# Projecting the second attention's queries, keys and values inside the first expert layer's loop, through one PSUM bank

## Chip, cores and metric

One NeuronCore of one Trainium2 chip runs the kernel. The metric is the device time of one execution in microseconds; the kernel before takes 853.91 us, the median of three runs (852.01 to 854.15).

## What is computed

4096 tokens (16 sequences of 256) of 128 features go through four layers, each with a residual and a normalisation behind it:

```python
x = _layernorm(x + _L0_attn_ref(x, ...))   # softmax attention, 16 heads of 8
x = _layernorm(x + _L0_ffn_ref(x, ...))    # 8 experts of 128, top 2, gated
x = _layernorm(x + _L1_attn_ref(x, ...))   # causal linear attention, Taylor feature map
x = _layernorm(x + _L1_ffn_ref(x, ...))    # 8 experts, each takes 512 tokens
```

The change touches the second and the third line. The second, for every token (clipping of gate and up left out):

```python
gate, up = gu[..., ::2], gu[..., 1::2]             # gu = x @ gate_up_proj + bias
act = (up + 1.0) * gate * sigmoid(gate * ALPHA)
out = sum over experts of w[token, e] * (act @ down_proj[e] + down_proj_bias[e])
```

The third begins with three projections of the normalised result: `q = x @ Wq.T` and `k = x @ Wk.T` (256 columns each, 16 heads of 16) and `v = x @ Wv.T` (128 columns).

## The kernel before

Tokens are processed in 8 chunks of 512 (`NCH`, `CH`), each of 4 tiles of 128 tokens. `xn` holds all tokens in SBUF, a tile per 128 columns. Every stage is a block with one instruction list per engine; each list runs strictly in the order written, and semaphores tie the lists together.

`expert_layer0` (line 339) runs 64 units, `n = 8 * chunk + expert`. On TensorE a unit is `expand(n)` (up, L466, then gate, L468, into two double-buffered banks) and `reduce(n - 2)` (the down projection of the unit two before, L478). At given units `turn_weights` and `add_bias` are put behind that, for the bias of the down projection; they use `ps_r` and `ps_d` in turn. ScalarE reads up (`take_up`, L701) and gate with the activation (`take_gate`, L706). VectorE's iteration n is `clip(n)`, `activate(n)` (L579), `accumulate(n - 2)` (L590, four instructions that add the weighted result into `xn`), and at some n `add_bias`, `row_stats` and `merge_rows` for the normalisation. GpSimd normalises a few tiles at the start of the stage (L746).

`project_layer1` (line 775) is the next stage. Per chunk: VectorE and GpSimd normalise the tiles (L864, L922), TensorE transposes them (`turn`, L843), ScalarE copies the result to `x2T` (L893), TensorE makes four projections of 128 columns (two for q, two for k; L853) into four banks and v into a fifth (L856). Each projection is split into three bf16 parts that sum to it: `hi` (ScalarE, L898), `residual` (VectorE, L871), `mid` (ScalarE, L902), `lo` (GpSimd, L927). SP stores the parts to `scratch_q` and `scratch_k` in DRAM (L826, one DMA per projection and chunk), laid out by chunk, `[NCH, 3, 256, 512]`. All four banks are in use at once: projection i of a chunk waits only for the residual of projection i of the chunk before.

`attend_taylor` (line 1879) then runs 32 units, each of 8 heads of one sequence. `load_slot` (L772) brings a unit's stacked parts from the scratch rows to SBUF, in 6 DMAs, into one of 4 slots (`BUFS1`); the first 2 (`AHEAD1`) are loaded by the stage before. TensorE's scores (L1952, L1956) wait for them, and SP's load into a slot waits for the scores that used it.

The reciprocal root of the normalisation is made on VectorE, for 24 tiles at once during the last units (`norm_out.seed_early`, `refine_early`) and for the last 8 at the start of `project_layer1` (`norm.invert_rest`).

Of the kernel before, what the change touches and what calls it, by code (L numbers as in the profile page):

```python
# [6 lines left out]
F32 = mybir.dt.float32  # L7
# [32 lines left out]
BUFS1, AHEAD1 = 4, 2  # L40
# [298 lines left out]
def expert_layer0(nc, xn, stats, norm, norm_out, consts):  # L339
# [3 lines left out]
    with ExitStack() as ctx:  # L343
# [25 lines left out]
        bns = sb("bns", [P, NTILE, 6])  # L369
        ps_g = [ps(f"ps_g{i}", [P, CH]) for i in range(2)]  # L370
# [3 lines left out]
        ps_bias = (ps_r, ps_d)  # L374
# [31 lines left out]
        s_bn = sem("row_stats_taken")  # L406
        groups = ((0, 2), (2, NCH))
        units = E * NCH
        turn_at = [E - 1] + [E * c + 2 for c in range(1, NCH)]
        bias_at = [E + 1] + [E * c + 4 for c in range(1, NCH)]  # L410
        with nc.Block() as block:  # L411
            @block.tensor
            def _(pe):
# [28 lines left out]
                def turn_weights(c):  # L442
                    pe.wait_ge(s_wt, 1 if c < groups[0][1] else 2)
                    after(pe, s_y, c - 1)
# [3 lines left out]
                    if c == 1:  # L448
                        pe.wait_ge(s_lk, NCH)
                    for t in range(4):  # L450
                        last = nc.tensor.transpose(ps_bias[c % 2][0:32, t * P:(t + 1) * P], wt[:, 4 * c + t, :], ident[:, :])
                    last.then_inc(s_wtp, 1)

                def add_bias(c):
                    pe.wait_ge(s_wT, c + 1)
                    for t in range(4):
                        here = slice(t * P, (t + 1) * P)
                        last = nc.tensor.matmul(ps_bias[c % 2][:, here], wT[:, c % 2, here], bd[:, :], start=True, stop=True)
# [11 lines left out]
                def reduce(n):  # L470
# [8 lines left out]
                    last.then_inc(s_dn, 1)  # L479

# [10 lines left out]
                for n in range(2, units):  # L491
# [10 lines left out]
                    if n in bias_at:  # L502
                        add_bias(bias_at.index(n))
                for n in (units - 2, units - 1):
                    reduce(n)

            @block.vector
            def _(ve):
# [85 lines left out]
                def add_bias(c, added):  # L594
                    ve.wait_ge(s_bm, c + 1)
                    ve.wait_ge(s_acc, added)
                    nc.vector.tensor_tensor(xn[:, 4 * c:4 * c + 4, :], ps_bias[c % 2][:, :].rearrange("p (t c) -> p t c", t=4),
# [9 lines left out]
                def merge_rows(c):  # L607
                    ve.wait_ge(s_bn, 4 * c + 4)
                    for t in range(4 * c, 4 * c + 4):
                        norm_out.merge(bns, t)  # L610
# [25 lines left out]
                for n in range(3, units):  # L636
# [19 lines left out]
                    if e == 3 and c > 0:  # L656
                        row_stats(c - 1)
                    if e == 7 and c > 0:
                        merge_rows(c - 1)
                    if n == E * (NCH - 1):  # L660
                        norm_out.seed_early(ve)
                    if E * (NCH - 1) < n <= E * (NCH - 1) + 3:
                        norm_out.refine_early(ve, n - E * (NCH - 1) - 1)
                for n in (units - 2, units - 1):
                    accumulate(n)
                row_stats(NCH - 1)
                merge_rows(NCH - 1)

            @block.scalar
            def _(act_e):  # L670
# [21 lines left out]
                def copy_weights(c):  # L692
# [3 lines left out]
                    nc.scalar.activation(wT[0:32, c % 2, :], ps_bias[c % 2][0:32, :], ACT.Copy).then_inc(s_wT, 1)  # L696
# [28 lines left out]
                for n in range(2, units):  # L725
# [12 lines left out]
                    if n in turn_at:  # L738
                        copy_weights(turn_at.index(n))

            @block.gpsimd
            def _(pool):
                for c in range(NCH):
# [8 lines left out]
def layer1_attention(nc, io, xn, stats, norm, norm_out, consts):  # L752

    scratch = [nc.dram_tensor(f"scratch1_{n}", [NCH, NPART, 2 * P, CH], BF16, kind="Internal").ap() for n in "qk"]
    with ExitStack() as keep:
        v_all = keep.enter_context(nc.sbuf_tensor("v_all1", [P, NTILE, H, HV], F32))
        stacks = [keep.enter_context(nc.sbuf_tensor(f"{n}st1", [P, BUFS1, UH, T], BF16)) for n in "qk"]  # L760
        wo = consts["later"]["wo1"]
        project_layer1(nc, stacks, scratch, v_all, xn, stats, norm, consts)
        attend_taylor(nc, stacks, scratch, v_all, xn, norm_out, consts, wo)

def load_slot(sp, u, stacks, scratch, done, names="qk"):

    h0, t0 = UH * (u % 2), T * ((u // 2) % 2)
    for name in names:
        st, sc = stacks["qk".index(name)], scratch["qk".index(name)]
        src = sc[u // 4, :, :, :].rearrange("s (d h) t -> (s d) h t", h=H)[:, h0:h0 + UH, t0:t0 + T]  # L770
        for s0, part, n in SLOT_RUNS[name]:
            sp.dma_start(st[FD * s0:FD * (s0 + n), u % BUFS1, :, :],  # L772
                         src[FD * part:FD * (part + n), :, :]).then_inc(done, 16)

def project_layer1(nc, stacks, scratch, v_all, xn, stats, norm, consts):

    ident = consts["ident"]
    with ExitStack() as ctx:
        def sb(name, shape, dt=F32):
            return ctx.enter_context(nc.sbuf_tensor(f"p1_{name}", shape, dt))  # L780

        def ps(name, shape, dt=F32):
            return ctx.enter_context(nc.psum_tensor(f"p1_{name}", shape, dt))

        phase = consts["semaphores"]

        def sem(name):
            return phase.take(f"p1_{name}")

# [1479 lines left out]
```

## Time and profile before

| | |
|---|---|
| median of three runs | 853.91 us (852.01 to 854.15) |
| the profiled execution's own time | 856.66 us |
| its span, first to last instruction | 854.9 us |
| busy: TensorE, VectorE, ScalarE, GpSimd | 663.0, 555.0, 432.2, 405.3 us |
| mean granted clock of TensorE | 0.896 |
| first expert layer | 249.6 (first up) to 441 us |
| projection of the second attention | 442 to 508 us |
| second attention | 508 to 658 us |

All times on the profile's axis are counted from the span's start. A clock of 1.00 is 2.4 GHz, 0.50 is 1.2 GHz. In a timeline, start and length come first, then the engine, the line, what is written and read, the shape and the count; brackets give the engine's idle time ahead of it and what ended that. Float32 products run as two passes, so each 512-column product counts two instructions. PE is the matmul side of TensorE, PEld its weight loads, DVE is VectorE, ACT ScalarE, POOL GpSimd.

### The profile page before, as it was taken

To read this page: it belongs to the slowest core of one execution; us is meant where nothing else is said; L and a number is where in the kernel's file an instruction comes from. 1 tells how busy PE (TensorE), PEld (TensorE's weight loads), DVE (VectorE), ACT (ScalarE), POOL (GpSimd) and SP (SyncE) were. 2 spreads that over 40 slices of the span, in tenths; PEclk is the share of its full clock that TensorE was granted. 3 is DMA by queue.
4 is the path that set the end of the run, shared out by engine and by line. 5 is a ranking of instruction groups with operands and counts; after the bars stand their busy time and mean duration, and the time that the engine had idled before them with its cause. 6 is when DMAs were issued, how large, how long until landed. Compare 5 with 4: busy or idle time off the path is not lost. (4 is left out here: it accounts for less than half of the span.)

```text
span 854.9 us, 18149 instructions
## 1 busy us (share of the span) xinstructions
PE 663.0 (78%) x6567; PEld 417.3 (49%) x6567; DVE 555.0 (65%) x1594; ACT 432.2 (51%) x627; POOL 405.3 (47%) x583
## 2 busy tenths in 40 slices
PE   6748999999869999999977669999896413888500
PEld 3423555555435666666644336766664103555400
DVE  6977888888468898888887643544456884222116
ACT  5433777777745555555526656766662600232102
POOL 7853777777640000000016756665564502788743
PEclk9975999999979999999989978999997755899765
DMA  4774463431000000000004999999991340355354
GB/s 159 244 221 94 135 169 97 120 95 54 4 1 1 1 1 2 1 1 1 2 0 177 264 257 174 189 178 173 187 183 55 91 114 17 74 129 98 34 94 124
DMA packets 134839, 85.76 MB, mean 100 GB/s; under 512 B 11104, under 2 KB 131424, under 8 KB 134624
## 3 DMA queue, kind: packets, MB, share of 16 engines
q1 hardware_dynamic: 127968, 79.30, 40.7%
q0 software_dynamic: 5632, 4.33, 3.7%
q8 instruction: 53, 0.87, 0.5%
q10 hardware_dynamic: 1152, 0.98, 0.4%
q14 instruction: 34, 0.28, 0.1%
HBM read 54.70 MB, written 29.49 MB: 98 GB/s over the span
## 5 line engine op out<-in xcount | busy, mean ns | idle before, releaser
L2120 ACT ACTIVATE a_prob<-a_ps_pair 128x1024 f32<-128x1024 f32 x96 | 93.8, 1023 | 51.9 <-PE a_ps_pair L1956 34.0
L1791 ACT ACTIVATE a_prob<-a_ps_pair 128x1024 f32<-128x1024 f32 x96 | 96.5, 1023 | 14.0 <-PE a_ps_pair L1594 10.9
L2132 POOL TENSOR_SCALAR_AFFINE_SELECT a_prob<-a_prob 128x512 f32<-128x512 f32 (+1 forms) x96 | 76.8, 805 | 55.0 <-ACT a_prob L2120 54.8
L1832 POOL TENSOR_SCALAR_AFFINE_SELECT a_prob<-a_prob 128x512 f32<-128x512 f32 (+1 forms) x96 | 75.4, 787 | 42.0 <-ACT a_prob L1791 41.3
L1730 DVE TENSOR_REDUCE a_mx<-a_ps_pair 128x4 f32<-128x1024 f32 x64 | 77.8, 1221 | 24.5 <-PE a_ps_pair L1635 22.8
L922 POOL TENSOR_SCALAR xn<-xn,stats,norm_b_rstd 128x128 f32<-128x128 f32 x8 | 6.4, 805 | 175.0 <-POOLq L411 175.0
L478 PEld LDWEIGHTS m_ps_n<-wd,m_act 128*128 128x128 f32 x512 | 66.4, 192 | 29.0 <-issue 27.4
L701 ACT ACTIVATE m_up<-m_ps_u,m_bup 128x512 f32<-128x512 f32 x64 | 44.0, 687 | 65.4 <-PE m_ps_u L466 65.3
L590 DVE SCALAR_TENSOR_TENSOR xn<-m_ps_n,m_wt,xn 128x128 f32<-128x128 f32 x256 | 71.7, 343 | 0.2 <-DVE xn L590 0.2
L478 PE MATMUL m_ps_n<-wd,m_act 128*128 128x128 f32 x512 | 67.6, 275 | 1.0 <-DVE xn L590 0.8
L466 PE MATMUL m_ps_u<-m_x1T,wgu 128*128 128x512 f32 x128 | 67.0, 606 | 0.0
L468 PE MATMUL m_ps_g<-m_x1T,wgu 128*128 128x512 f32 x128 | 65.4, 592 | 0.0
L1376 ACT ACTIVATE c_hT<-c_ps_x,c_w 128x512 f32<-128x512 f32 x16 | 11.0, 687 | 101.2 <-PE c_ps_x L1195 101.2
L1409 POOL DMA_INDIRECT sum<-c_o,c_idx x32 | 50.5, 1579 | 15.5 <-issue 9.0
L579 DVE SCALAR_TENSOR_TENSOR m_act<-m_glu,m_upc 128x512 f32<-128x512 f32 x64 | 44.3, 693 | 15.7 <-ACT m_glu L706 13.2
L1401 POOL DMA_INDIRECT c_y<-normed,c_idx x32 | 31.0, 970 | 47.9 <-DVE c_idx L1298 38.4
L706 ACT ACTIVATE m_glu<-m_ps_g,bgu 128x512 f32<-128x512 f32 x64 | 44.0, 687 | 10.6 <-PE m_ps_g L468 10.6
L927 POOL TENSOR_TENSOR p_parts<-p_resid,p_parts 128x512 bf16<-128x512 f32 x32 | 37.0, 1169 | 18.0 <-ACT p_parts L902 18.0
L1952 PE MATMUL a_ps_pair<-qst,kst 96*128 96x256 bf16 x256 | 37.0, 282 | 7.9 <-DMA kst<-scratch_k 5.4
L1733 DVE TENSOR_REDUCE a_mx<-a_ps_pair 128x8 f32<-128x1024 f32 x32 | 39.2, 1225 | 2.3 <-PE a_ps_pair L1635 1.0
L1304 DVE COPY c_kept<-c_y 128x4 f32<-128x4 f32 x8 | 1.6, 205 | 58.6 <-PE c_ps_x L1186 58.6
L468 PEld LDWEIGHTS m_ps_g<-m_x1T,wgu 128*128 128x128 f32 x128 | 24.5, 191 | 30.9 <-issue 30.9
(287 smaller groups left out, 1525.8 us busy)
## 6 DMA issues: line engine op xcount, KB each, us to landing
qst<-scratch_q SPq DMA_DIRECT2D x64, 128.0 KB, 4.2
kst<-scratch_k SPq DMA_DIRECT2D x64, 128.0 KB, 4.2
scratch_q<-p_parts SPq DMA_DIRECT2D x16, 384.0 KB, 3.1
scratch_k<-p_parts SPq DMA_DIRECT2D x16, 384.0 KB, 2.8
qst<-scratch_q SPq DMA_DIRECT2D x32, 192.0 KB, 6.1
kst<-scratch_k SPq DMA_DIRECT2D x32, 192.0 KB, 6.0
c_w<-in_w SPq DMA_DIRECT2D x8, 578.0 KB, 4.0
scratch_q<-parts SPq DMA_DIRECT2D x16, 256.0 KB, 2.5
```

The source lines that it names most:

```text
L466: nc.tensor.matmul(ps_u[n % 2][:, :], wgu[:, e, 1, :], xc, start=True, stop=True).then_inc(s_u, 1)
L468: nc.tensor.matmul(ps_g[n % 2][:, :], wgu[:, e, 0, :], xc, start=True, stop=True).then_inc(s_g, 1)
L478: last = nc.tensor.matmul(ps_n[n % 2][:, here], act[:, n % ABUFS, here], wd[:, e, :], start=True, stop=True)
L579: nc.vector.scalar_tensor_tensor(act[:, n % ABUFS, :], glu[:, n % 2, :], GLU_LIMIT, upc[:, n % 2, :], ALU.min, ALU.mult)\
L590: last = nc.vector.scalar_tensor_tensor(y, ps_n[n % 2][:, t * P:(t + 1) * P], wt[:, 4 * c + t, e:e + 1], y, ALU.mult, ALU.add)
L701: nc.scalar.activation(up[:, n % 2, :], ps_u[n % 2][:, :], ACT.Identity, bias=bup[:, n % E:n % E + 1]).then_inc(s_uc, 1)
L1409: nc.gpsimd.indirect_dma_start(out=sum_d, out_offset=bass.IndirectOffsetOnAxis(ap=idx[:, a, e:e + 1], axis=0), in_=o[:, e % 2, a, :], in_o ...
L1730: nc.vector.reduce_max(mx[:, w % 2, :, 2 * f:2 * f + 2, 1:2], pair[p][:, :].rearrange("p (m h k) -> p m h k", m=2, h=2), AX_X).then_inc(s_ ...
L1791: nc.scalar.activation(prob[:, r % 6, :], pair[(0, 2, 1)[j]][:, :], ACT.Exp, scale=scale, bias=0.0).then_inc(s_e, 1)
L1832: nc.gpsimd.affine_select(out=blk, in_=blk, compare_op=ALU.is_ge, fill=0.0, base=0, pattern=[[0, n], [1, P]], channel_multiplier=-1).then_ ...
L2120: nc.scalar.activation(prob[:, r % 6, :], pair[r % 2][:, :], ACT.Square, scale=scale, bias=1.0).then_inc(s_e, 1)
L2132: nc.gpsimd.affine_select(out=blk, in_=blk, compare_op=ALU.is_ge, fill=0.0, base=0, pattern=[[0, n], [1, P]], channel_multiplier=-1).then_ ...
```

## The change

The stage `project_layer1` is gone. Its work is moved into `expert_layer0`: a chunk is projected while later chunks go through the experts. `stats_at`, `next_at` and `next_steps` say in which units: for chunk c, row statistics in unit 8c+9, the seeds of the root on VectorE in 8c+10, and from unit 8c+12 on six steps, one behind each unit: the transposes, four projections, v. The last chunk (`tail`) comes after the loop.

- The transposes, the four projections and v of a chunk go through one bank, `ps_d`; the last chunk's projections have four. `turn_weights` and `add_bias` use `ps_r` alone, at other units than before.
- The refinement of the root is done per chunk on GpSimd (`refine_root`), which also normalises two of the four tiles; ScalarE does the other two (`renormalise`). v is copied by ScalarE instead of VectorE.
- There are 2 buffers for the residuals where there were 4, and 4 for the parts where there were 8.
- The scratch rows are laid out by sequence, `[NB, 3, 256, 256]`. A store becomes two DMAs; in a load, the 8 heads of a row lie one behind another in DRAM.
- `AHEAD1` is 4: all four slots are loaded in the expert stage, behind the stores of chunk 1 and the next.

```diff
-BUFS1, AHEAD1 = 4, 2
+BUFS1, AHEAD1 = 4, 4
+PBUFS = 4
...
-        ps_bias = (ps_r, ps_d)
...
-        turn_at = [E - 1] + [E * c + 2 for c in range(1, NCH)]
-        bias_at = [E + 1] + [E * c + 4 for c in range(1, NCH)]
+        turn_at = [E - 2] + [E * c + 3 for c in range(1, NCH)]
+        bias_at = [E - 1] + [E * c + 5 for c in range(1, NCH)]
+        stats_at = [E * c + E + 1 for c in range(NCH - 1)]
+        next_at = [E * c + E + 4 for c in range(NCH - 1)]
+        tail = NCH - 1
+        next_steps = {n0 + i: (c, i) for c, n0 in enumerate(next_at) for i in range(6)}
+        def projected(n):
+            return ps_d if n // 4 < tail else (ps_g + ps_u)[n % 4]
...
+            @block.sync
+            def _(sp):
+                for n in range(4 * NCH):
+                    c, i = n // 4, n % 4
+                    sp.wait_ge(s_lo, n + 1)
+                    half = P * (i % 2)
+                    for b in range(2):
+                        sp.dma_start(scratch[i // 2][2 * c + b, :, half:half + P, :].rearrange("s p t -> p s t"),
+                                     parts[:, n % PBUFS, :, T * b:T * b + T]).then_inc(s_store[n % PBUFS], 16)
+                    if 7 <= n < 7 + AHEAD1:
+                        if n == 7:
+                            for k in range(4):
+                                sp.wait_ge(s_store[k], 32)
+                        load_slot(sp, n - 7, stacks, scratch, s_first)
...
             @block.tensor
+                def turn_next(c):
+                    pe.wait_ge(s_x2a, 2 * c + 2)
+                    pe.wait_ge(s_x2p, 2 * c + 2)
+                    if c == 0:
+                        pe.wait_ge(s_lk, NCH)
+                    after(pe, s_vc, c)
+                    if c == tail:
+                        pe.wait_ge(s_y, NCH)
+                    out = ps_d if c < tail else ps_r
+                    for t in range(4):
+                        last = nc.tensor.transpose(out[:, t * P:(t + 1) * P], xn[:, 4 * c + t, :], ident[:, :])
+                    last.then_inc(s_xp2, 1)
+                def project(n):
+                    c, i = n // 4, n % 4
+                    pe.wait_ge(s_xT2, c + 1)
+                    if c < tail:
+                        after(pe, s_r1, n if i else 0)
+                    nc.tensor.matmul(projected(n)[:, :], wqk[:, i, :], x2T[:, c % 2, :], start=True, stop=True).then_inc(s_proj, 1)
+                def project_v(c):
+                    pe.wait_ge(s_xT2, c + 1)
+                    if c < tail:
+                        pe.wait_ge(s_r1, 4 * c + 4)
+                    else:
+                        pe.wait_ge(s_vc, c)
...
                         add_bias(bias_at.index(n))
+                    if n in next_steps:
+                        next_layer(*next_steps[n])
                 for n in (units - 2, units - 1):
                     reduce(n)
+                for n in range(units, max(next_steps) + 1):
+                    next_layer(*next_steps[n])
+                turn_next(tail)
+                for i in range(4):
+                    project(4 * tail + i)
+                project_v(tail)
             @block.vector
+                def residual(n):
+                    ve.wait_ge(s_hi, n + 1)
+                    after(ve, s_lo, n - 1)
+                    nc.vector.tensor_tensor(resid[:, n % 2, :], projected(n)[:, :], level(n, 0), ALU.subtract).then_inc(s_r1, 1)
...
                     accumulate(n - 2)
...
+                    if n - 1 in next_steps and 1 <= next_steps[n - 1][1] < 5:
+                        residual(4 * next_steps[n - 1][0] + next_steps[n - 1][1] - 1)
                     if n - 1 in bias_at:
                         add_bias(bias_at.index(n - 1), n - 1)
+                    if n in stats_at:
+                        row_stats(stats_at.index(n))
+                    if n - 1 in stats_at:
+                        seed_root(stats_at.index(n - 1))
                 for n in (units - 2, units - 1):
                     accumulate(n)
+                row_stats(tail)
+                seed_root(tail)
+                for n in range(units - 1, max(next_steps) + 1):
+                    if 1 <= next_steps[n][1] < 5:
+                        residual(4 * next_steps[n][0] + next_steps[n][1] - 1)
+                for i in range(4):
+                    residual(4 * tail + i)
             @block.scalar
+                def next_layer(c, i):
+                    if 2 <= i:
+                        mid(4 * c + i - 2)
+                    if i == 0:
+                        copy_x2(c)
+                    elif i < 5:
+                        hi(4 * c + i - 1)
+                    else:
+                        copy_v(c)
...
                         copy_weights(turn_at.index(n))
+                    if n in next_at:
+                        renormalise(next_at.index(n))
+                    if n in next_steps:
+                        next_layer(*next_steps[n])
...
             @block.gpsimd
+                def refine_root(c):
+                    h = slice(4 * c, 4 * c + 4)
+                    v, t, r = var2[:, h], root[:, h], rstd2[:, h]
+                    pool.wait_ge(s_seed, 3 * c + 3)
+                    for turn in range(3):
+                        step(nc.gpsimd.tensor_tensor(t, r, r, ALU.mult))
+                        step(nc.gpsimd.tensor_tensor(t, t, v, ALU.mult))
+                        step(nc.gpsimd.tensor_scalar(t, t, -0.5, 1.5, ALU.mult, ALU.add))
+                        step(nc.gpsimd.tensor_tensor(r, r, t, ALU.mult))
+                    step(nc.gpsimd.tensor_scalar(t, r, -1.0, None, ALU.mult))
+                    nc.gpsimd.tensor_tensor(shift2[:, h], t, stats[:, h, 0], ALU.mult).then_inc(s_sh2, 1)
+                    for t in (4 * c + 2, 4 * c + 3):
+                        nc.gpsimd.tensor_scalar(xn[:, t, :], xn[:, t, :], stats[:, t, 0:1], rstd2[:, t:t + 1],
+                                                ALU.subtract, ALU.mult).then_inc(s_x2p, 1)
+                for c in range(NCH):
+                    refine_root(c)
+                    for i in range(4):
+                        lo(4 * c + i)
...
+def load_slot(sp, u, stacks, scratch, done):
+    h0 = UH * (u % 2)
+    for st, sc, runs in zip(stacks, scratch, (SLOT_RUNS["q"], SLOT_RUNS["k"])):
+        src = sc[u // 2, :, :, :].rearrange("s (d h) t -> (s d) h t", h=H)[:, h0:h0 + UH, :]
+        for s0, part, n in runs:
+            sp.dma_start(st[FD * s0:FD * (s0 + n), u % BUFS1, :, :], src[FD * part:FD * (part + n), :, :]).then_inc(done, 16)
```

## Rows read from the trace of the kernel before

**Rows 1.** Stretches: length; busy PE, PEld, DVE, ACT, POOL; PEclk; DMA share; GB/s.

```profile
306.00:394.00 88.00, 88.00 (x429) 57.42 (x428) 75.11 (x236) 45.89 (x68) 0.00 (x0) 1.00 0.00 1
...
250.00:433.60 183.60, 181.51 (x924) 117.22 (x924) 156.13 (x497) 98.94 (x155) 4.45 (x6) 1.00 0.00 1
433.60:508.10 74.50, 48.54 (x190) 28.43 (x190) 48.87 (x108) 40.74 (x75) 44.12 (x41) 0.90 0.63 191
508.10:658.30 150.20, 135.77 (x1792) 95.68 (x1792) 70.38 (x289) 93.79 (x96) 84.49 (x129) 0.95 1.04 159
```

**Rows 2.** Timeline of the last two units of the expert layer.

```profile
431.02 1.02 PE L466 MATMUL m_ps_u<-m_x1T,wgu 128*128 128x512 f32 x2
...
433.63 1.02 PE L466 MATMUL m_ps_u<-m_x1T,wgu 128*128 128x512 f32 x2
...
434.49 1.02 PE L468 MATMUL m_ps_g<-m_x1T,wgu 128*128 128x512 f32 x2
...
435.55 0.69 ACT L706 ACTIVATE m_glu<-m_ps_g,bgu 128x512 f32<-128x512 f32 x1 [0.17 <-PE m_ps_g L468]
...
436.27 0.69 DVE L579 SCALAR_TENSOR_TENSOR m_act<-m_glu,m_upc 128x512 f32<-128x512 f32 x1 [0.20 <-ACT m_glu L706]
...
436.88 1.12 DVE L590 SCALAR_TENSOR_TENSOR xn<-m_ps_n,m_wt,xn 128x128 f32<-128x128 f32 x4
```

**Rows 3.** Groups by line, 442 to 507 us: busy, mean ns | idle before.

```profile
L927 POOL TENSOR_TENSOR p_parts<-p_resid,p_parts 128x512 bf16<-128x512 f32 x32 | 37.0, 1169 | 18.0 <-ACT p_parts L902 18.0
L853 PE MATMUL p_ps_qk<-p_x2T,wqk 128*128 128x512 f32 x64 | 31.9, 647 | 0.0
L871 DVE TENSOR_TENSOR p_resid<-p_ps_qk,p_parts 128x512 f32<-128x512 f32 x32 | 21.4, 686 | 19.0 <-ACT p_parts L898 19.0
L902 ACT ACTIVATE p_parts<-p_resid 128x512 bf16<-128x512 f32 x32 | 19.9, 629 | 4.5 <-DVE p_resid L871 4.5
```

**Rows 4.** Timeline of TensorE, projection stage and start of the attention.

```profile
443.36 1.10 PE L843 MATMUL p_ps_x<-ident,xn 128*128 128x128 f32 x4 [4.09 <-DVE xn L864]
...
461.38 0.63 PE L843 MATMUL p_ps_x<-ident,xn 128*128 128x128 f32 x4 [2.27 <-issue]
461.85 5.29 PE L853 MATMUL p_ps_qk<-p_x2T,wqk 128*128 128x512 f32 x8
...
508.10 0.77 PE L1964 MATMUL a_ps_z<-v_all,upper 128*128 128x128 f32 x2 [7.60 <-PEq L817]
```

**Rows 5.** A stretch behind the gap at 461 us, columns as in rows 1.

```profile
462.60:466.00 3.40, 3.40 (x5) 1.35 (x4) 1.36 (x3) 1.90 (x4) 1.03 (x2) 0.51 0.65 232
```

**Rows 6.** Timeline of GpSimd: small dependent steps, and one tile normalised.

```profile
163.04 0.22 POOL L1842 TENSOR_TENSOR a_mres<-a_mx,a_mparts 128x16 f32<-128x16 f32 x1
163.33 0.20 POOL L1844 CAST a_mparts<-a_mres 128x16 bf16<-128x16 f32 x1
163.60 0.22 POOL L1846 TENSOR_TENSOR a_mparts<-a_mres,a_mparts 128x16 bf16<-128x16 f32 x1
...
460.50 0.79 POOL L922 TENSOR_SCALAR xn<-xn,stats,norm_b_rstd 128x128 f32<-128x128 f32 x1
```

**Rows 7.** Timeline: the first and the last chunk of the projection.

```profile
444.50 0.60 ACT L893 ACTIVATE p_x2T<-p_ps_x 128x512 f32<-128x512 f32 x1 [8.26 <-PE p_ps_x L843]
...
446.06 5.06 PE L853 MATMUL p_ps_qk<-p_x2T,wqk 128*128 128x512 f32 x8
...
448.01 0.60 ACT L898 ACTIVATE p_parts<-p_ps_qk 128x512 bf16<-128x512 f32 x1 [2.92 <-PE p_ps_qk L853]
...
496.02 3.60 PE L853 MATMUL p_ps_qk<-p_x2T,wqk 128*128 128x512 f32 x8
...
500.05 4.49 POOL L927 TENSOR_TENSOR p_parts<-p_resid,p_parts 128x512 bf16<-128x512 f32 x4 [0.36 <-ACT p_parts L902]
```

**Rows 8.** Attention, 510 to 655 us: longest wait for loads, and packets moved.

```profile
PEld a_ps_pair L1952 <- DMA kst<-scratch_k: 7.0, 7, 1.3
...
DMA packets 48547, 23.67 MB, mean 163 GB/s; under 512 B 2871, under 2 KB 48526, under 8 KB 48526
```

More of the change, by code:

```diff
@@ L369, in expert_layer0 @@
         bns = sb("bns", [P, NTILE, 6])
+        wqk, wv1 = consts["later"]["wqk1"], consts["later"]["wv1"]
+        var2, root, rstd2, shift2 = [sb(n, [P, NTILE]) for n in ("var2", "root", "rstd2", "shift2")]
+        x2T = sb("x2T", [P, 2, CH])
+        resid = sb("resid", [P, 2, CH])
+        parts = sb("parts", [P, PBUFS, NPART, CH], BF16)
         ps_g = [ps(f"ps_g{i}", [P, CH]) for i in range(2)]
@@ L407, in expert_layer0 @@
+        s_lo = sem("lo_done")
+        s_store = [sem(f"parts_stored{i}") for i in range(PBUFS)]
+        s_first = sem("first_stacks_loaded")
+        s_vp = sem("v_projected")
+        s_vc = sem("v_copied")
+        s_ones = sem("ones_set")
         groups = ((0, 2), (2, NCH))
         units = E * NCH
-        turn_at = [E - 1] + [E * c + 2 for c in range(1, NCH)]
-        bias_at = [E + 1] + [E * c + 4 for c in range(1, NCH)]
-        with nc.Block() as block:
+        turn_at = [E - 2] + [E * c + 3 for c in range(1, NCH)]
@@ L443, in turn_weights @@
                     pe.wait_ge(s_wt, 1 if c < groups[0][1] else 2)
-                    after(pe, s_y, c - 1)
+                    after(pe, s_y, c)
                     if c == 0:
@@ L457, in add_bias @@
                         here = slice(t * P, (t + 1) * P)
-                        last = nc.tensor.matmul(ps_bias[c % 2][:, here], wT[:, c % 2, here], bd[:, :], start=True, stop=True)
+                        last = nc.tensor.matmul(ps_r[:, here], wT[:, c % 2, here], bd[:, :], start=True, stop=True)
                     last.then_inc(s_bm, 1)
@@ L479, in reduce @@
                     last.then_inc(s_dn, 1)
+                def turn_next(c):
[22 more added lines that the diff above has]
+                        pe.wait_ge(s_vc, c)
+                    for t in range(4):
+                        here = slice(t * P, (t + 1) * P)
+                        last = nc.tensor.matmul(ps_d[:, here], x2T[:, c % 2, here], wv1[:, :], start=True, stop=True)
+                    last.then_inc(s_vp, 1)
+                def next_layer(c, i):
+                    if i == 0:
+                        turn_next(c)
+                    elif i < 5:
+                        project(4 * c + i - 1)
+                    else:
+                        project_v(c)
                 turn_x(0)
@@ L739, in _ @@
                         copy_weights(turn_at.index(n))
+                    if n in next_at:
+                        renormalise(next_at.index(n))
+                    if n in next_steps:
+                        next_layer(*next_steps[n])
+                for n in range(units, max(next_steps) + 1):
+                    next_layer(*next_steps[n])
+                renormalise(tail)
+                copy_x2(tail)
+                hi(4 * tail)
+                for n in range(4 * tail + 1, 4 * tail + 4):
+                    hi(n)
+                    mid(n - 1)
+                copy_v(tail)
+                mid(4 * tail + 3)
             @block.gpsimd
@@ L750, in _ @@
                         nc.gpsimd.memset(wT[:, :, :], 0.0).then_inc(s_wTz, 1)
[L752 to L763, printed above, removed]
@@ new lines, in _, with step @@
+                nc.gpsimd.memset(v_all[:, :, :, HD:HV], 1.0).then_inc(s_ones, 1)
+                done = [0]
+                def step(ins):
+                    done[0] += 1
+                    ins.then_inc(s_root, 1)
+                    pool.wait_ge(s_root, done[0])
+                def refine_root(c):
+                    h = slice(4 * c, 4 * c + 4)
+                    v, t, r = var2[:, h], root[:, h], rstd2[:, h]
[10 more added lines that the diff above has]
+                                                ALU.subtract, ALU.mult).then_inc(s_x2p, 1)
```

242 lines of the change are left out of this document (69 added, 173 removed).

## Prediction

> **What bounds the kernel now.** I read the busy shares by stage first [rows 1]. In the first expert layer (250 to 433.6 us) TensorE is busy 88.0 of 88 us in its middle part at granted clock 1.00, while VectorE is busy 75.1, ScalarE 45.9 and GpSimd nothing. The projection of the second attention, with the end of the expert layer before it, fills 433.6 to 508.1: TensorE 48.5 of 74.5 us, DMA 0.63. The attention itself (508.1 to 658.3) has TensorE busy 136 of 150 us and a DMA share of 1.04. The chain of waits reaches back only to 658 us, so for these stages it says nothing; they are read from the order of the queues and from single units.
>
> Next, one unit of the expert layer [rows 2]. Unit n is up, gate, then `reduce(n-2)` on TensorE, which takes its work strictly in order. Up starts at 431.02 and 433.63: 2.61 us a unit. Gate starts 0.86 after up, so two passes over 512 columns cost 0.86 and eight over 128 columns the remaining 0.89. The other engines follow. Counted from up's start: the gate's ScalarE work starts at +1.92 (435.55), VectorE's activation at +2.64 (436.27), its four accumulations for unit n-2 at +3.25 (436.88), done at +4.37. VectorE thus ends an iteration 1.8 us after TensorE has left the unit. Today that costs nothing, because TensorE needs the result only units later.
>
> **The change part by part.** *Work added to TensorE.* Per chunk, 4 transposes (0.47, from 461.38 to 461.85 [rows 4]), 4 projections of 0.86 and 8 passes for v (0.89): 4.80 us. TensorE has no free time to take it in. Up to the start of unit 63, six whole chunks and the transposes and two projections of the seventh are done: 6 x 4.80 + 2.19 = 31.0.
>
> *The wait that the one bank brings.* `project(n)` waits for `residual` of the projection before, since both use `ps_d`. It stands in TensorE's unit n behind `reduce(n-2)`; the residual stands in VectorE's iteration n behind `accumulate(n-2)`. So TensorE can't come to it late enough: VectorE ends accumulating at +4.37 and needs 0.69 for the residual [rows 3], +5.06; with 0.05 for the signal (an estimate) TensorE goes on at +5.1, where it was ready at +2.61. That is a stall of 2.5, with the whole expert loop queued behind it. It can't be caught up: the next unit's residual again needs that unit's own gate, activation and reduction. Three projections and the v step of a chunk wait in this way, the first projection doesn't. Before unit 63 starts: 6 x 4 + 1 = 25 stalls, 62.5 us. Bounds: 2.2 (accumulate bound by the reduction instead of the activation) to 2.8.
>
> *The root on GpSimd.* `turn_next` waits for tiles that GpSimd renormalises after 14 small steps, each waiting for the one before. Nearest rows: small dependent steps start every 0.28 [rows 6], so 3.9; the 3 seed steps on VectorE at the same pace, 0.84; two tiles of 0.79, 1.6 [rows 6]. From the start of unit 8c+10: VectorE free at 4.37, seed 5.2, root 9.1, tiles 10.7. TensorE arrives after 2.61 + 3.08 (with the weights' transposes, 0.47) + 2.61 = 8.3 and waits 2.4. Bounds: 0, if the steps on 4 columns are faster than these on 16, to 4. Seven times: 16.8. ScalarE waits for the root at the same point; what is queued behind it, the next unit's up and gate, can't start earlier than the stalled TensorE anyway.
>
> *The other engines.* VectorE gains 4 residuals a chunk (2.8) and loses the normalising; its 88 - 75.1 = 12.9 us free per four chunks [rows 1] cover it. ScalarE (hi, mid, two copies, two tiles, about 7 us a chunk) has half its time free. GpSimd was idle. The stores, now two per part, and the loads of four slots stand on SP, which has nothing else there, and the DMA share there is 0.00. These are zero; without the cover the largest, VectorE's 2.8 a chunk, would be 20.
>
> *The clock.* Gaps of 4.09 and 7.60 on TensorE were followed by matmuls at half speed, and of the six gaps between chunks of the projection (up to 2.27) one was, the one at 461.38 [rows 4]: 0.51 over 3.4 us [rows 5], where eight passes took 5.29 instead of 3.60, 1.7 lost. My gaps (from the reduction's modelled end at +2.77 to +5.1) are 2.3 long, so I take one in six of 33: 5.5 x 1.7 = 9. Bounds: none, and all 33, 56.
>
> *The end of the expert layer and the projection.* What stays is a chain for the last chunk. From the start of unit 63: third projection done at 6.0, two reductions 7.7, their accumulations 9.5 (VectorE, with one 0.2 step), row statistics 10.8, seed 11.7, residual 12.4. TensorE has been idle for over 4 us, so it is cold: hi starts 1.95 after the projection does (446.06 to 448.01 [rows 7]), then hi 0.6, residual 0.69, mid 0.63, lo 1.17 [rows 3, 7]: 17.4. GpSimd begins the last root only after that lo: 21.4, tiles 22.9, cold transposes 1.1, copy 0.6 [rows 4, 7]: 24.7. From the first projection of a chunk to its last lo 8.5 us pass (496.02 to 504.54 [rows 7]), cold 0.9 more: 34.1; from there to the next stage 3.6 (504.54 to 508.10 [rows 4, 7]): 37.7. Before it took 508.10 - 433.63 = 74.5. Saved: 36.8.
>
> *Scratch rows by batch.* A load's eight heads become one run of 4 KB where they were runs of 512 B. TensorE waited 7.0 us for them in the attention [rows 8]. The queue moved packets of 488 B on average there (23.67 MB in 48547), 159 GB/s at share 1.04, against 191 GB/s at 0.63 in the stage before, which mostly stores runs of 1 KB [rows 1, 8]: longer runs move about twice as much per busy time. I take 6 of the 7; bounds 0 and 10. AHEAD1 of 4 lands two more slots before the stage and is in this term.
>
> The Trainium skill's page "DMA: Bandwidth & Descriptors" (Specifications) gives 512 B as the shortest transfer that reaches line rate. By it the old loads were there already, the 6 us wouldn't come and the sum would be 6 higher; the two shares above speak against it, though one stage mostly loads and the other mostly stores.
>
> *Sum.* 31.0 + 62.5 + 16.8 + 9 - 36.8 - 6 = +76.5. The profiled execution took 856.66 us (span 854.9), 2.75 above the median of the three runs, 853.91. With the change: 933.2 profiled, 930.4 as a median.
>
> **The rivals.** *Faster: the stalls don't come.* If VectorE had the residual ready when TensorE comes back, the 25 stalls, the 16.8 and the clock's 9 fall away, and 2.5 more in unit 63: 31.0 - 39.3 - 6 = -14.3, about 840. For it: VectorE has 12.9 us free in four chunks and runs no other long work. Against it: not its load but its place in the order decides, and the order puts the residual behind the accumulation of the unit that TensorE has just reduced. It decides at 14.3 / 32, a gap of 0.45 us: below it the change gains.
>
> *The clock falls at every gap.* Then 56 in place of 9: +123.5, 977. For it: gaps this long now come every 6 us, where they came every 7.2. Against it: five of six gaps in the projection, about as long, left the clock at 1.00.
>
> *The root is hidden and the clock stays.* GpSimd's steps on 4 columns may take half of those on 16; then 16.8 and 9 fall away: +50.7, 905.
>
> *The change doesn't do what it says.* If the loads stay slow because of their 96 rows and not because of short runs, 6 us are missing: 936, inside the range.
>
> **How the numbers follow.** Forecast 0.68, clock at every gap 0.14, root hidden 0.11, faster 0.07. The predicted time is the first, 930. The range goes from the case with the root hidden (905, less 1) up to near the case of the clock (975) and leaves out the gain and half of the clock's case. Differences under 0.3% (2.6 us) can't be told from none here; only a gap within 0.1 us of 0.45 would give that, 0.01. Faster 0.07, slower 0.92.
>
> **What would show it.** Right, if the unit's start to start in the profile after is 2.61 without a step and about 6.0 with a waiting step, TensorE's idle time before the `project` line is near 2.4 a time and released by VectorE's residual, TensorE's share in the expert layer falls from 100% to about 70%, and the next attention starts some 80 us later than at 508. The root's term is right if `turn_next` waits some 2 us for GpSimd's tiles. The row change is right if the DMA waits before L1952's matmuls are gone. It would be wrong if TensorE's queue showed no idle time ahead of the projections, or if its clock stood at half for long stretches.

## The result, and the profile after

The kernel with the change takes 964.78 us, the median of four executions (963.85 to 970.30); the one before took 854.03 beside it. The ratio is 1.132 (95% interval 1.128 to 1.136). The profiled execution took 964.76 us, its span is 963.0: 108.1 more than before. The prediction was 930 with a range of 904 to 975, and 933.2 for the profiled execution: the result lies inside the range, sign and mechanism came out, but the cost was 32 us higher than the forecast.

TensorE's queue in three units of chunk 1 and one without a step, for comparison with [rows 2] (start, length, engine, line, operation, in brackets idle time and what ended it):

```profile
360.42 1.10 PE L548 MATMUL m_ps_d<-m_x2T,wqk 128*128 128x512 f32 x2 [2.34 <-DVE m_resid L721]
361.36 1.02 PE L515 MATMUL m_ps_u<-m_x1T,wgu 128*128 128x512 f32 x2
...
366.47 1.10 PE L548 MATMUL m_ps_d<-m_x2T,wqk 128*128 128x512 f32 x2 [2.34 <-DVE m_resid L721]
367.40 1.02 PE L515 MATMUL m_ps_u<-m_x1T,wgu 128*128 128x512 f32 x2
...
372.51 1.83 PE L548 MATMUL m_ps_d<-m_x2T,wqk 128*128 128x512 f32 x2 [2.34 <-DVE m_resid L721]
374.13 1.91 PE L515 MATMUL m_ps_u<-m_x1T,wgu 128*128 128x512 f32 x2
375.84 1.18 PE L517 MATMUL m_ps_g<-m_x1T,wgu 128*128 128x512 f32 x2
...
381.21 1.02 PE L515 MATMUL m_ps_u<-m_x1T,wgu 128*128 128x512 f32 x2
...
383.82 1.02 PE L515 MATMUL m_ps_u<-m_x1T,wgu 128*128 128x512 f32 x2
...
392.82 0.73 PE L540 MATMUL m_ps_d<-ident,xn 128*128 128x128 f32 x4 [3.18 <-ACT xn L815]
```

A unit that waits takes 367.40 - 361.36 = 6.04 from up to up, one without a step 2.61, as before. The third projection shown shows the clock: after the same wait its two passes and up's take 1.83 and 1.91 us instead of 1.10 and 1.02, and the granted clock from 372.6 to 376 is 0.52. Such a stretch is called half speed below. The last line is `turn_next`, which waits for the renormalised tiles.

By stage (length; busy PE, PEld, DVE, ACT, POOL; granted clock; DMA share; GB/s): two chunks of the loop, unit 63 up to the attention, and the attention, to be read against [rows 1]:

```profile
337.19:381.21 44.02, 31.49 (x130) 19.11 (x129) 21.74 (x66) 18.56 (x29) 10.12 (x21) 0.92 0.13 36
381.21:426.00 44.79, 32.25 (x130) 19.86 (x129) 21.82 (x66) 18.56 (x29) 10.89 (x21) 0.90 0.43 106
...
583.60:621.92 38.32, 16.97 (x62) 10.02 (x60) 10.82 (x32) 12.06 (x21) 13.12 (x24) 0.73 0.29 82
...
622.00:766.30 144.30, 133.00 (x1792) 94.35 (x1792) 71.37 (x290) 92.87 (x96) 84.42 (x129) 0.97 0.63 155
```

A chunk of eight units took 22.2 before, at clock 1.00 (from 355.67 to 377.88; no idle time in 88 us, [rows 1]); now 44 to 45, of which TensorE is idle 12.5. Unit 63 begins at 583.60 instead of 433.63, the attention at 621.92 instead of 508.10.

### The profile page after: what moved, and what is told of

Its sections match the earlier page's. It is cut to its first block and busy times, and to the rows that moved or that the text cites. A ratio compares the mean times of both kernels' runs of the same rounds, so it can differ in the third digit from the quotient of the medians.

```text
span 963.0 us, 18313 instructions
## 1 busy us (share of the span) xinstructions
PE 694.0 (72%) x6567; PEld 431.1 (45%) x6567; DVE 537.9 (56%) x1562; ACT 446.7 (46%) x651; POOL 442.1 (46%) x703
## 5 line engine op out<-in xcount | busy, mean ns | idle before, releaser
L940 POOL TENSOR_TENSOR m_parts<-m_resid,m_parts 128x512 bf16<-128x512 f32 x32 | 36.8, 1154 | 206.3 <-ACT m_parts L830 206.3
L669 DVE TENSOR_SCALAR m_upc<-m_up 128x512 f32<-128x512 f32 x64 | 27.4, 428 | 130.1 <-ACT m_up L851 130.1
L515 PE MATMUL m_ps_u<-m_x1T,wgu 128*128 128x512 f32 x128 | 79.4, 708 | 0.0
L548 PE MATMUL m_ps_d<-m_x2T,wqk 128*128 128x512 f32 x56 | 37.3, 754 | 51.1 <-DVE m_resid L721 51.1
L517 PE MATMUL m_ps_g<-m_x1T,wgu 128*128 128x512 f32 x128 | 69.3, 624 | 0.0
L830 ACT ACTIVATE m_parts<-m_resid 128x512 bf16<-128x512 f32 x32 | 20.1, 629 | 68.9 <-DVE m_resid L721 68.9
L517 PEld LDWEIGHTS m_ps_g<-m_x1T,wgu 128*128 128x128 f32 x128 | 27.8, 217 | 38.5 <-issue 38.5
```

Of the source, the lines that this page charges most:

```text
L515: nc.tensor.matmul(ps_u[n % 2][:, :], wgu[:, e, 1, :], xc, start=True, stop=True).then_inc(s_u, 1)
L517: nc.tensor.matmul(ps_g[n % 2][:, :], wgu[:, e, 0, :], xc, start=True, stop=True).then_inc(s_g, 1)
```

## The experiments

*First: is it the place of the residual, the clock, or the rows?* Four kernels tell them apart; the kernel before took 852.72 beside them.

**The residual first.** The changed kernel, but the residual opens VectorE's iteration instead of standing behind the accumulations:

```diff
+                    if n - 1 in next_steps and 1 <= next_steps[n - 1][1] < 5:
+                        residual(4 * next_steps[n - 1][0] + next_steps[n - 1][1] - 1)
                     clip(n)
...
-                    if n - 1 in next_steps and 1 <= next_steps[n - 1][1] < 5:
-                        residual(4 * next_steps[n - 1][0] + next_steps[n - 1][1] - 1)
                     if n - 1 in bias_at:
```

> The kernel after, with VectorE's residual at the start of its iteration (ahead of clip) instead of behind the accumulation; the same work, the same one bank. My theory, TensorE's projections wait for VectorE's place in the order: the 27 gaps of 2.34 us before the projections and v vanish (25 x 2.5 us before unit 63, 2.5 in it), and with them the nine falls of the clock that follow them (9 x 1.7); the gap before the transposes (9.0 once, 3.2 six times) stays with its own falls. 964.8 - 65 - 15 = 885, range 870 to 895. Rival, the units are long because the added work is too much for VectorE and ScalarE: then the gaps only move, and the time stays above 940.

881.78 us, ratio to before 1.034 (1.031 to 1.036). Moving two lines takes 83 us off. No gap stands ahead of a projection or v in the loop any more; `turn_next` still waits, 8.96 in chunk 0 and 3.2 to 3.5 in each of the others, and five of these seven gaps are followed by half speed. A projection, v and the next turn:

```profile
313.61 1.02 PE L548 MATMUL m_ps_d<-m_x2T,wqk 128*128 128x512 f32 x2
...
324.02 1.06 PE L558 MATMUL m_ps_d<-wv,m_x2T 128*128 128x128 f32 x8
...
336.53 1.09 PE L540 MATMUL m_ps_d<-ident,xn 128*128 128x128 f32 x4 [3.19 <-ACT xn L815]
```

The one bank is thus no cost by itself: the same bank, the same work and the same chain, but with the residual early enough.

**Two banks.** The projections use `ps_d` and `ps_r` in turn, the residual stays at the end of the iteration. (Not shown: the bias, which also uses `ps_r`, is added one unit earlier, and further waits guard that bank.)

```diff
-            return ps_d if n // 4 < tail else (ps_g + ps_u)[n % 4]
+            return (ps_d, ps_r)[n % 2] if n // 4 < tail else (ps_g + ps_u)[n % 4]
...
-                    after(pe, s_r1, n if i else 0)
+                    elif i > 1:
+                        pe.wait_ge(s_r1, n - 1)
```

> The kernel after, with its order on VectorE, but the projections of a chunk in turn through two banks (the other one is that of the bias, whose addition is moved one unit ahead), so that each waits for the residual before the last. My theory, it is the one bank that ties the projection to a residual which the order puts too late: the gaps before the projections and v vanish as with the residual first, 870 to 895. Rival, the place of the residual alone is at fault and a second bank doesn't help: above 940. A second rival, both are needed: in between, 900 to 940.

915.37, ratio 1.073 (1.070 to 1.076): 20 us above the theory's upper end, and inside the range of the second rival, though not for its reason. The projections' gaps are gone here too, except for 0.96 ahead of v, but the wait has moved. TensorE's timeline:

```profile
341.24 1.08 PE L543 MATMUL m_ps_d<-ident,xn 128*128 128x128 f32 x4 [5.32 <-ACT xn L821]
360.95 1.13 PE L564 MATMUL m_ps_d<-wv,m_x2T 128*128 128x128 f32 x8 [0.96 <-DVE m_resid L727]
369.69 1.13 PE L529 MATMUL m_ps_n<-wd,m_act 128*128 128x128 f32 x8 [0.23 <-DVE xn L692]
377.03 1.08 PE L543 MATMUL m_ps_d<-ident,xn 128*128 128x128 f32 x4 [5.32 <-ACT xn L821]
```

TensorE no longer waits for VectorE, so VectorE lags behind it, and the seed of the root at the end of a late iteration comes later still: it begins 7.5 behind the start of its unit on TensorE (326.13 to 333.66) instead of 4.3 (337.19 to 341.48 in the changed kernel). `turn_next` now waits 5.32 instead of 3.18, and all seven turns' gaps are followed by half speed. More space let TensorE run ahead and changed nothing in VectorE's order.

**The rows alone.** The kernel before, with only the scratch rows laid out by sequence:

```diff
-    scratch = [nc.dram_tensor(f"scratch1_{n}", [NCH, NPART, 2 * P, CH], BF16, kind="Internal").ap() for n in "qk"]
+    scratch = [nc.dram_tensor(f"scratch1_{n}", [NB, NPART, 2 * P, T], BF16, kind="Internal").ap() for n in "qk"]
...
-                        dst = scratch[i // 2][c, :, half:half + P, :].rearrange("s p t -> p s t")
-                        sp.dma_start(dst, parts[:, n, :, :]).then_inc(s_store[n], 16)
+                        for b in range(2):
+                            dst = scratch[i // 2][2 * c + b, :, half:half + P, :].rearrange("s p t -> p s t")
+                            sp.dma_start(dst, parts[:, n, :, T * b:T * b + T]).then_inc(s_store[n], 16)
```

> The kernel before, with the scratch rows by sequence alone (stores in two DMAs, loads of runs of 4 KB); AHEAD1 stays 2 and the projection stays a stage of its own. My theory, the load's short runs bound the attention's DMA: the seven waits for loads (7.0 us) are gone, DMA share in the attention falls from 1.04 to about 0.65, 848 (846 to 850). Rival, the 5.9 us that the attention became shorter came from the four slots loaded ahead: 854. Second rival, the stores of half the run length delay the projection by as much: 854 too, but with the waits gone and the stage ahead longer.

853.21, ratio 0.9993 (0.9976 to 1.0009): no difference that can be measured. The attention does get shorter:

```profile
510.49:654.50 144.01, 133.07 (x1792) 94.52 (x1792) 70.25 (x288) 92.91 (x96) 84.07 (x129) 0.97 0.70 166
```

144.0 instead of 150.2, at a DMA share of 0.70 instead of 1.04 [rows 1], and without the waits for loads of [rows 8]. `AHEAD1` is 2 here, so it is not the slots loaded ahead. But the attention begins 2.4 later, at 510.49; 0.5 of that stood already at the last chunk's first projection (496.51 instead of 496.02). So part of the gain is given back ahead of it, as the second rival said; the second group comes back to that.

**The gaps filled.** The changed kernel, with two products that nothing uses (into `ps_r`) ahead of three of a chunk's four waits:

```diff
+                def fill(c):
+                    pe.wait_ge(s_y, c + 2)
+                    for i in range(2):
+                        nc.tensor.matmul(ps_r[:, :], wqk[:, i, :], x2T[:, c % 2, :], start=True, stop=True)
...
+                        if i >= 2:
+                            fill(c)
```

> The kernel after, with two more products of 512 columns (four passes, 1.7 us at full clock) on TensorE ahead of three of the four waits of a chunk (third and fourth projection, v); they go to the bank of the bias and nobody reads them. Theory that the gaps of 2.34 us let the clock fall: 8 of the 9 falls behind such gaps follow the filled ones, so 8 x 1.7 = 14 us are won, 951 (945 to 956), although TensorE has more work. Rival, the falls have nothing to do with these gaps: 965 or more.

955.18, ratio 1.120 (1.117 to 1.123): 9.6 us less than the changed kernel, although TensorE does more. Two turns, then a wait left open and a filled one:

```profile
347.34 0.63 PE L540 MATMUL m_ps_d<-ident,xn 128*128 128x128 f32 x4 [3.19 <-ACT xn L823]
...
387.81 1.09 PE L540 MATMUL m_ps_d<-ident,xn 128*128 128x128 f32 x4 [3.18 <-ACT xn L823]
...
400.58 2.05 PE L555 MATMUL m_ps_d<-m_x2T,wqk 128*128 128x512 f32 x2 [2.34 <-DVE m_resid L729]
405.74 1.88 PE L546 MATMUL m_ps_r<-m_x2T,wqk 128*128 128x512 f32 x4
408.15 1.13 PE L555 MATMUL m_ps_d<-m_x2T,wqk 128*128 128x512 f32 x2 [0.53 <-DVE m_resid L729]
```

The filled waits are 0.53 long, 19 in the loop, and none was followed by half speed; of the open ones of 2.34, four of seven were (in the changed kernel one of the same seven). The two turns waited equally long; behind 387.81 and three more of the seven the matmuls ran at half speed, behind 347.34 and two more they did not. The chunks whose turn was followed by half speed are the same four whose open wait was. A gap's length alone does not decide. The time lies in the expected range partly by luck: eight stretches of half speed are left of 16, as expected, but not the expected eight, and the four behind turns cost 2.8 to 2.9 each.

*Second: what is left of the loss when the order is mended?* These three share runs of before of 852.46.

**Residual and turn.** As the first, and the root's seed is made in the iteration of the row statistics, with the six steps one unit later (two in chunk 0; the last unchanged):

```diff
-        next_at = [E * c + E + 4 for c in range(NCH - 1)]
+        next_at = [E + 6] + [E * c + E + 5 for c in range(1, NCH - 2)] + [E * (NCH - 1) + 4]
...
-                    if n - 1 in stats_at:
-                        seed_root(stats_at.index(n - 1))
+                        seed_root(stats_at.index(n))
```

> The changed kernel with both of its waits shortened: the residual stands at the head of VectorE's iteration (as in e1_residual_first), and the seed of the root is taken in the same iteration as the row statistics while turn_next comes one or two units later (two for chunk 0). Theory (the loss is nothing but the order: residual behind the accumulations, 25 gaps, and a root that starts too late, 7 gaps, and the clock that falls after them): no gap ahead of L548, L558 or L540 in the loop, so the loop costs the 31 us of TensorE's work alone and the end of the two stages gives some 39 back: 840 to 845, below the kernel before. Rival (the work itself, spread over the loop, slows the other engines or the clock, whatever the order): 870 to 880, no better than e1_residual_first by more than a few us.

859.21, ratio 1.009 (1.006 to 1.013): neither theory: 14 us above the first's upper end and 11 below the rival's lower one. Most of the gaps are gone, as the first said; the rest is seen in the trace:

```profile
376.83 1.13 PE L558 MATMUL m_ps_d<-wv,m_x2T 128*128 128x128 f32 x8 [0.88 <-DVE m_resid L721]
404.92 1.13 PE L558 MATMUL m_ps_d<-wv,m_x2T 128*128 128x128 f32 x8 [0.88 <-DVE m_resid L721]
...
498.46 1.08 PE L540 MATMUL m_ps_r<-ident,xn 128*128 128x128 f32 x4 [5.21 <-POOL xn L934]
```

The row statistics of the next chunk now stand ahead of the last residual (0.88 a chunk), and the last chunk's turn still waits for GpSimd, whose root begins at 492.91 behind two `lo` steps, while VectorE had the seed by 487.6. The clock is 1.00 throughout the loop.

**The turn alone.** The same edit, with the residual left behind the accumulations.

> The changed kernel with only the seed and the place of turn_next mended; the residual stays behind the accumulations. Theory (7 gaps of 28.1 us in all, each with a half-speed stretch of 1.7): 965 - 28 - up to 12 = 925 to 937, and the 2.34 gaps ahead of each projection stay. Rival (the root's start is tied to VectorE, which lags because of the waits themselves): the gaps come back at another place and it stays above 950.

935.12, ratio 1.099 (1.094 to 1.104), inside the range: 29.7 below the changed kernel, about the 28.1 that the turns' gaps add up to. The turns' gaps are now 1.39 at most, and none is followed by half speed; nearly every 2.34 ahead of a projection stays, and now 12 of 25 are followed by half speed, where 9 of 26 were.

**One store again.** The rows by sequence in the kernel before, but the tile holds the two sequences' parts one behind the other, so that one DMA stores a part:

```diff
-                        for b in range(2):
-                            dst = scratch[i // 2][2 * c + b, :, half:half + P, :].rearrange("s p t -> p s t")
-                            sp.dma_start(dst, parts[:, n, :, T * b:T * b + T]).then_inc(s_store[n], 16)
+                        dst = scratch[i // 2][2 * c:2 * c + 2, :, half:half + P, :].rearrange("b s p t -> p (b s) t")
+                        sp.dma_start(dst, parts[:, n, :, :]).then_inc(s_store[n], 16)
```

> The kernel before with the scratch rows laid out by batch, as e3_layout_only, but each part is stored by one DMA and not by two (the two batches' rows stand behind each other in the tile). Theory (the loads gain 6 us and the doubled stores give 2.4 of it back on the way to the next stage): attention starts at 508 and not at 510.5, and the time is 2.4 below e3_layout_only's, 849 to 851. Rival (the later start comes from elsewhere, say from where the rows lie in memory): 853, as e3_layout_only.

853.62, ratio 1.0007 (0.9987 to 1.0027), as the rival said: the number of DMAs is not what eats the gain. The DMA share and rate at the end of the projection are (columns as above), before, with two stores, and with one:

```profile
498.00:505.00 7.00, 2.51 (x12) 1.43 (x10) 3.31 (x6) 4.34 (x9) 6.18 (x6) 0.90 1.03 352
```

```profile
498.00:505.00 7.00, 3.00 (x13) 1.62 (x11) 3.79 (x6) 4.83 (x9) 6.64 (x6) 0.91 1.00 283
```

```profile
498.00:505.00 7.00, 2.50 (x12) 1.43 (x10) 3.29 (x6) 4.33 (x9) 6.17 (x6) 0.89 1.05 308
```

The DMA engines are full in all three, and move 352 GB/s in runs of 1 KB, 283 and 308 in runs of 512 B. The layout took the short runs from the loads and gave them to the stores, which are the bound just there; the attention begins at 510.49 and 509.56 instead of 508.10. Each span is about 3 us below the profiled one of before, which itself was 2.75 above its median; so the medians differ by less than 1.2. How much of the 6 us in the attention belongs to that one execution of before is not settled.

*Third: can the order be mended to the end?* The kernel before took 853.61 beside each.

**Later v, early last root.** On top of residual and turn: v one unit later, the last chunk's root on GpSimd ahead of two `lo` steps, ScalarE's last tiles ahead of its copy of v.

```diff
-        next_steps = {n0 + i: (c, i) for c, n0 in enumerate(next_at) for i in range(6)}
+        next_steps = {n0 + i + (i == 5 and c < NCH - 2): (c, i) for c, n0 in enumerate(next_at) for i in range(6)}
...
+                    if n == 4 * tail - 2:
+                        refine_root(tail)
```

> e5_both with the two places mended that its trace still shows: the v step comes one unit later (0.88 of waiting in each of seven chunks, since VectorE's row statistics of the next chunk stand ahead of the last residual), and on GpSimd the last chunk's root stands ahead of the two last steps of the chunk before it (it began at 492.91, while VectorE had its seed ready at 487.6), with ScalarE's two last tiles ahead of its copy of v. Theory (what is left is a matter of order): 5 x 0.88 = 4.4 and some 4 to 5 less, 849 to 851, a little below the kernel before (852.5). Rival (the end is bound by the stores, whose traffic has to pass before the attention starts): the loop's 4.4 alone, 855.

869.92, ratio 1.017 (1.014 to 1.021): a miss by 19, and slower than without it. From unit 63's start to the last `lo` it takes 27.3 instead of 32.6, as expected. But the later v delays ScalarE's last `mid` of a chunk and with it GpSimd's last `lo`; behind that stands the next chunk's root, and the turns wait again, four times 2.02 or 2.03, once 3.39 and once 5.13, with half speed behind five of these six:

```profile
394.32 0.63 PE L541 MATMUL m_ps_d<-ident,xn 128*128 128x128 f32 x4 [2.03 <-ACT xn L815]
425.17 0.63 PE L541 MATMUL m_ps_d<-ident,xn 128*128 128x128 f32 x4 [2.02 <-ACT xn L815]
```

**Each root ahead of the last `lo`.** One more edit, on GpSimd:

```diff
+                refine_root(0)
                 for n in range(4 * NCH):
-                    if n % 4 == 0 and n < 4 * tail:
-                        refine_root(n // 4)
+                    if n % 4 == 3 and n // 4 < tail - 1:
+                        refine_root(n // 4 + 1)
```

> As e8_early_tail, but on GpSimd each chunk's root stands ahead of the last of the four `lo` steps of the chunk before. In e8_early_tail the later v step made that last `lo` later and with it the root behind it, so that turn_next waited 2.02 (five times, 3.39 and 5.13 once each), with half-speed stretches behind some of them, while the end of the layer did get shorter by 5.3 (from unit 63's start to the last `lo` 27.3 instead of 32.6). Theory (GpSimd's order was the cause): the 2.02 and the half-speed stretches go, each chunk takes 27.0 to 27.3, the shorter end stays: 845 to 850, below the kernel before. Rival (the later v step costs elsewhere, say on ScalarE, where the renormalising waits): the waits stay and it remains above 860.

846.48, ratio 0.9915 (0.9889 to 0.9942): faster than the kernel before by 0.6 to 1.1%, and far faster than the changed one.

```profile
365.00:420.00 55.00, 55.00 (x265) 35.53 (x264) 45.49 (x130) 36.66 (x60) 22.28 (x40) 1.00 0.40 104
```

TensorE has no idle time in these 55 us, at full clock, and a chunk takes 447.95 - 420.98 = 26.97: the 22.2 of before and the 4.8 of the projection's work. The change as planned costs its work and no more, if every engine's order fits.

## Why the prediction was right, and 32 us too low

Up to the start of unit 63 the sum was 31.0 + 62.5 + 16.8 + 9 = 119.3; it is 583.60 - 433.63 = 150.0. Term by term:

| term | predicted | measured |
|---|---|---|
| work on TensorE | 31.0 | 4.8 a chunk (26.97 less 22.2 where nothing waits): as predicted |
| 25 stalls | 62.5, 2.5 each | 64.3: (6.04 - 2.61 - 0.86) = 2.57 each |
| turn | 16.8 | 28.1: 8.96 once and 3.18 or 3.19 six times |
| clock | 9 | 26.5: 16 stretches at half speed, 1.3 to 2.7 each, mostly 1.5 to 1.7 |
| end of the layer and projection | 37.7 long | 38.3 |
| rows by batch, in the attention | -6 | -5.9 (150.2 to 144.3, one execution each) |

The clock's 26.5 are read from start to start, against the same stretch without half speed: 2.65 from a late projection to the reduction behind it (2.68 for v), and 3.97 from a turn to its first projection (347.34 to 351.31 in the kernel with the gaps filled). The measured terms of the loop make 149.9. Its units also start 0.8 earlier than before (unit 10 at 284.69 instead of 285.47); the 0.9 that this leaves is not assigned.

**Right: the stall.** It was worked out from one unit and from the order of two queues, and the first experiment shows its cause: with two lines moved all 26 waits of 2.34 ahead of projections and v are gone. The faster rival put the point of decision at a gap of 0.45; the gaps were 2.34.

**Undersized: the clock.** The prediction took one fall in six gaps from the projection stage [rows 4, 5]. A stretch at half speed cost 1.66 on average, close to the 1.7 taken, but there were 16 of them and not 5.5. Here each of the seven turns' gaps was followed by half speed, which the count of 33 gaps "2.3 long" had not in it as a class of its own, and 9 of the 26 waits of 2.34: one in three, not one in six. The granted clock of a chunk fell to 0.90 to 0.92, in chunk 0 to 0.84. That no filled gap was followed by half speed shows that this is the gaps' doing. The step that failed is the frequency: six gaps of another stage, with other work around them, were too few to take it from. Nor is there one frequency to take: for the same 2.34 it was 9 of 26 here, 4 of 7 with the others filled, and 12 of 25 with the turn mended. The bound of 56 for all of them held.

**Undersized: the turn.** Of the 11.3 us, about 5 are six times 0.8. GpSimd's 14 steps take 3.86 alone, as predicted (601.19 to 605.05, at the end, where VectorE is idle), but 5.0 in the loop; VectorE's seed, done 4.85 behind the start of its unit (342.04 against 337.19) and not 5.2, gives 0.3 of that back. GpSimd and VectorE side by side:

```profile
342.51 0.71 POOL L929 TENSOR_TENSOR m_root<-m_root,m_var 128x4 f32<-128x4 f32 x1
343.32 0.19 POOL L930 TENSOR_SCALAR m_root<-m_root 128x4 f32<-128x4 f32 x1
...
344.71 0.40 POOL L931 TENSOR_TENSOR m_rstd<-m_rstd,m_root 128x4 f32<-128x4 f32 x1
...
345.75 0.51 POOL L930 TENSOR_SCALAR m_root<-m_root 128x4 f32<-128x4 f32 x1
```

```profile
342.48 0.69 DVE L675 SCALAR_TENSOR_TENSOR m_act<-m_glu,m_upc 128x512 f32<-128x512 f32 x1
343.08 1.12 DVE L686 SCALAR_TENSOR_TENSOR xn<-m_ps_n,m_wt,xn 128x128 f32<-128x128 f32 x4
344.63 0.43 DVE L669 TENSOR_SCALAR m_upc<-m_up 128x512 f32<-128x512 f32 x1 [0.42 <-ACT m_up L851]
345.49 0.72 DVE L675 SCALAR_TENSOR_TENSOR m_act<-m_glu,m_upc 128x512 f32<-128x512 f32 x1 [0.43 <-ACT m_glu L856]
```

The steps that take 0.40 to 0.71 instead of 0.20 end at 343.22, 345.11 and 346.26, each 0.05 behind the end of VectorE's clip or activation (343.17, 345.06, 346.21). During the accumulations, which read PSUM, they keep their 0.20. The Trainium skill's page "SBUF — State Buffer" (SBUF: two separate sides) says that the two engines share a pair of ports, which one instruction holds to its end when VectorE reads two SBUF operands or runs in its two-port mode; the trace agrees, and the prediction would have been nearer with it. No run here tested it by itself. The other part, 8.96 - 2.4 = 6.6, is chunk 0: there VectorE picks the second experts for the router in the same iterations, ahead of the seed, so that the root begins at 295.08 while TensorE is ready at 293.35 (its last reduction starts at 292.22 and takes 1.13):

```profile
294.03 0.36 DVE L650 TENSOR_TENSOR m_route<-m_route,m_pick 128x192 f32<-128x192 f32 x1
294.42 0.17 DVE L711 TENSOR_SCALAR m_var<-stats 128x4 f32<-128x4 f32 x1
```

```profile
295.08 0.31 POOL L928 TENSOR_TENSOR m_root<-m_rstd 128x4 f32<-128x4 f32 x1 [27.62 <-DVE m_rstd L715]
```

```profile
302.31 1.09 PE L540 MATMUL m_ps_d<-ident,xn 128*128 128x128 f32 x4 [8.96 <-ACT xn L815]
```

The prediction had taken one chunk for all seven.

**Right in size in one execution, open in worth: the rows.** The waits and the 6 us went as forecast, with a DMA share of 0.63 in place of 1.04, read against the one profiled execution of before, which was 2.75 above its median. In the kernel before the same layout brings nothing measurable: part is lost at the end of the projection, where the DMA engines are full and the stores now move the short runs; the rest is the open point above, and the medians do not show that the 6 us are won. In the changed kernel most stores lie in the loop at a share of 0.13 to 0.43, and no engine waits for a DMA there. The Trainium skill's page "DMA: Bandwidth & Descriptors" (Specifications), which the prediction weighed, has the line rate from 512 B on. The measurement of stores differs and decides: with the engines full, 1 KB runs moved 352 GB/s and 512 B runs 283 to 308.

## What to carry to other kernels

When a stage is woven into another's loop, write down for each engine at which point of the iteration it does the new step, and at which point the strict queue of the bound engine comes for it: here two lines in VectorE's order were worth 83 us, and a further bank, without that, less. After each mended wait look for the next queue that is late, GpSimd's too, until the bound engine shows no idle time; the same weaving then went from 13% slower to about 0.9% faster. Look at the odd chunks, first and last, by themselves.

## What the runs showed of the hardware

TensorE's clock fell from 2.4 to 1.2 GHz behind gaps of 2.34 us in 9 of 26 cases in the changed kernel, in 4 of 7 with the other gaps filled and in 12 of 25 with the turn mended; behind gaps of 3.18 or 3.19 in all of six in the changed kernel, but in three of six with the gaps filled and three of five with the residual first; behind gaps of 2.02 or 2.03 in three of four with the later v; behind the 19 gaps of 0.53 it never fell. What decides between equal gaps is not settled. A stretch cost 1.3 to 2.9 us. Small GpSimd steps were held up until a VectorE instruction of 0.4 to 0.7 us had ended. Changing the run length of a store from 1 KB to 512 B cost 12 to 20% of the rate with the DMA engines full (308 and 283 GB/s for 352).
